# A two-batch attention and expert layer on one core: the stage ahead of the first pair of heads is reordered

## The reference

```
n  = layernorm(x)
q, k, v = n @ wq, n @ wk, n @ wv              # 16 heads of 64
s  = q k^T + bias[bucket(key - query), head]  # 2048 x 2048 for each batch and head
a  = softmax(s) v @ wo
x  = x + layernorm(a)
f  = layernorm(x);  gates = top-2 softmax of mean(f) @ gate_w^T + gate_b
x  = x + layernorm(sum over 8 experts of gate_e * gelu(f @ expert_w_e^T + expert_b_e))
```

## Time and profile before

| | us |
|---|---|
| median of 3 runs | 3034.44 (3033.16 to 3037.01) |
| profiled execution | 3035.34 |
| its span | 3033.6 |
| PE busy | 2843.5 (94%) |
| POOL busy | 2276.8 (75%) |
| DVE busy | 1852.2 (61%) |
| ACT busy | 1663.9 (55%) |

### The profile page before, as it was taken

How to read it: one execution, slowest core, us unless ns; L and a number is a source line. 1 busy time by engine, 2 the same in 40 slices (tenths; PEclk the granted TensorE clock), 3 DMA queues, 4 the chain that set the end, 5 groups by cost and what they waited for, 6 DMA issues and landing times.

```text
span 3033.6 us, 49858 instructions
## 1 busy us (share of the span) xinstructions
PE 2843.5 (94%) x18785; PEld 1052.1 (35%) x18785; DVE 1852.2 (61%) x4692; ACT 1663.9 (55%) x2174; POOL 2276.8 (75%) x1033
## 2 busy tenths in 40 slices
PE   3499999999999999999999999999999999988887
PEld 2133333333333333333333333333333333322443
DVE  5465656665566656565666556565656666685676
ACT  2255555555655555555555565556555555566576
POOL 0088888888888888888988888888888888987000
PEclk8599999999999999999999999999999999999998
DMA  7000000000000000000000000000000000100001
GB/s 159 23 1 1 1 1 18 1 1 1 19 1 1 1 3 17 2 1 2 19 2 1 1 19 1 2 1 2 19 1 1 1 8 1 57 1 29 1 1 56
DMA packets 45607, 36.53 MB, mean 12 GB/s; under 512 B 21510, under 2 KB 43782, under 8 KB 45366
## 3 DMA queue, kind: packets, MB, share of 16 engines
q1 hardware_dynamic: 45366, 33.34, 4.2%
HBM read 28.39 MB, written 11.34 MB: 13 GB/s over the span
## 4 chain that ended last, share of the span: by engine, by line
PE 48%; DVE 20%; issue 18%; POOL 9%; ACT 4%; DMA 1%; SPq 1%; POOLq 0%; DVEq 0%; ACTq 0%
PE po L617 16%; PE st L587 14%; POOL acc L527 9%; PE pre L599 5%; DVE mpart L1265 4%; PE pm L555 4%; DVE st L1282 3%; PE st L817 3%; DVE pre L1262 3%; PE pm L561 2%; DVE pre L1257 2%; PE pm L647 2%; ACT prob L896 1%; PE pm L626 1%; DMA t_scratch<-w_scratch 1%
## 5 line engine op out<-in xcount | busy, mean ns | idle before, releaser
L527 POOL TENSOR_TENSOR acc<-acc,prob 128x1024 f32<-128x1024 f32 x896 | 2117.3, 2363 | 388.1 <-ACT prob L896 308.2
L896 ACT ACTIVATE prob<-st 128x1024 f32<-128x1024 f32 x1024 | 1016.6, 1022 | 911.7 <-DVE st L1282 813.8
L617 PE MATMUL po<-prob,v 128*64 128x512 f32 x4096 | 994.9, 606 | 0.0
L587 PE MATMUL st<-qk 64*128 64x512 f16 x6144 | 835.4, 378 | 21.3 <-ACT prob L896 16.7
L1257 DVE CUSTOM_DVE_ANT_0 pre<-pre,ew 128x512 f32<-128x512 f32 x448 | 300.8, 713 | 567.0 <-issue 566.9
L1262 DVE CUSTOM_DVE_ANT_0 pre<-pre,tab 128x512 f32<-128x512 f32 x704 | 475.2, 715 | 147.2 <-issue 147.1
L587 PEld LDWEIGHTS st<-qk 64*128 64x128 f16 x6144 | 293.3, 94 | 349.9 <-ACT prob L896 60.2
L617 PEld LDWEIGHTS po<-prob,v 128*64 128x64 f32 x4096 | 249.0, 136 | 442.0 <-issue 367.5
L587 PE MATMUL st<-eq,ek 64*128 64x512 f16 x2048 | 389.8, 377 | 0.0
L599 PE MATMUL pre<-qk 64*128 64x512 f16 x1600 | 311.9, 386 | 52.9 <-ACT ew L926 19.2
L1265 DVE TENSOR_REDUCE mpart<-pre 128x2 f32<-128x1024 f32 x224 | 274.0, 1223 | 98.4 <-PE pre L599 96.8
(11 more groups left out here) (189 smaller groups left out, 2350.6 us busy)
## 6 DMA issues: line engine op xcount, KB each, us to landing
t_scratch<-w_scratch SPq DMA_DIRECT2D x2, 3072.0 KB
inv_r<-inv SPq DMA_DIRECT2D x260, 1.0 KB, 1.7
y<-x SPq DMA_DIRECT2D x2, 2048.0 KB, 11.5
qk<-x SPq DMA_DIRECT2D x8, 512.0 KB, 5.6
out<-qk SPq DMA_DIRECT2D x8, 512.0 KB, 3.5
w<-w_pairs SPq DMA_DIRECT2D x8, 384.0 KB, 3.7
t2f<-t_scratch SPq DMA_DIRECT2D x8, 384.0 KB, 4.8
t<-t_scratch SPq DMA_DIRECT2D x8, 384.0 KB, 3.2
```

The lines of the kernel that those rows point to most:

```text
L527: nc.gpsimd.tensor_tensor(acc[g % 2][:, :, :], a, prob[:, n % RING, :, :], ALU.add).then_inc(sum_p, 1)
L587: last = nc.tensor.matmul(st[:, 2 * (n % 2) + h, :], w[64 * h:64 * h + 64, :], t[64 * h:64 * h + 64, :], start=(r == 0), stop=(r == len(te ...
L617: last = nc.tensor.matmul(po[64 * h:64 * h + 64, :], v[:, g // CHUNKS, j, 64 * h:64 * h + 64], prob[:, n % RING, h, :], start=(s == 0), st ...
L896: nc.scalar.activation(prob[:, n % RING, :, :], st[:, 2 * (n % 2):2 * (n % 2) + 2, :], ACT.Exp).then_inc(exp_done, 1)
```

## The change

- SP issues the small loads first, then batch 0's x in four parts with a semaphore each, weights and identity. Batch 1's x is issued when the bias by distance has been stored. Of the tables the first pair's two heads are made first, each table by a DMA of its own, and `t2f` is loaded as soon as its own is there; the fourteen other heads follow. The repetition of two heads at the end of each table is no longer made. Waits for the rest of the tables are put in `tables_in` for pairs 0 and 1.
- DVE takes the statistics of batch 0 part by part, and normalises two of its four groups; ACT normalises the other two and all of batch 1 (`first_tokens`, with a bias made by one more small operation). Batch 1's statistics are put between the low parts of batch 0.
- The first four projections are the key chunks, each when its 512 tokens are there, in the banks `pre`, `po` and `pm`, then query chunk 0 in `st`. The other seven (three query, four value chunks) stand behind pieces 1, 3, 5, 7, 8, 9 and 10 (`FILL_ORDER`, `FILL_AT`). Batch 1's transposes, high and low tokens are put between pieces 11 to 15.
- The far rows and the pair table are made ahead of piece 6.
- y is not cleared: group 0's addition is left out, and the first eight groups write y instead of adding to it.
- The columns' sums on ACT and the memsets at the end of each normalisation go.

```diff
+FILL_ORDER = [4, 5, 6, 7, 0, 1, 2, 3, 8, 9, 10, 11]
+FILL_AT = {1: 5, 3: 6, 5: 7, 7: 8, 8: 9, 9: 10, 10: 11}
...
@@ block.sync
-            for b in range(B):
-                sp.dma_start(y[:, TT * b:TT * b + TT, :], x[b, :, :].rearrange("(t p) d -> p t d", p=128)).then_inc(x_in[b], 16)
...
+            sp.dma_start(hot, onehot).then_inc(rel_in, 16)
+            sp.dma_start(rowc[:, :], rows).then_inc(rel_in, 16)
+            for g in range(GROUPS):
+                sp.dma_start(y[:, 4 * g:4 * g + 4, :], x[0, QC * g:QC * g + QC, :].rearrange("(t p) d -> p t d", p=128)).then_inc(x_part[g], 16)
             sp.dma_start(w3[:, :, :, :].rearrange("p n k c -> p (n k c)"), w_pairs[0, :, :]).then_inc(w_in, 16)
+            sp.dma_start(ident[:, :], eye).then_inc(ident_in, 16)
+
+            def table_out(n, first, heads, done):
+                src = w_scratch[:, n, 127:127 + BAND]
+                src = bass.AP(src.tensor, src.offset + 1024 * first, [[1024, heads], [-1, 128], [1, BAND]])
+                sp.dma_start(t_scratch[n, first:first + heads, :, :], src).then_inc(done, 16)
+
+            sp.wait_ge(dist_out, 2)
+            sp.dma_start(w_scratch, by_dist).then_inc(scratch_out, 16)
+            sp.dma_start(y[:, TT:2 * TT, :], x[1, :, :].rearrange("(t p) d -> p t d", p=128)).then_inc(x_in, 16)
+            sp.wait_ge(scratch_out, 16)
+            table_out(1, 0, 2, first_out)
+            sp.wait_ge(first_out, 16)
+            sp.dma_start(t2f[:, :, :], t_scratch[1, 0:2, :, :].rearrange("h p u -> p h u")).then_inc(t2_in, 16)
+            table_out(0, 0, 2, first_out)
...
             for n in range(2):
-                for to, heads in ((0, H), (H, 2)):
...
+                table_out(n, 2, H - 2, tables_out)
...
@@ block.tensor
+            pe.wait_ge(ident_in, 16)
+            transposes(0, 0)
+            transposes(0, 1)
...
+            for n in range(4):
+                pe.wait_ge(xh_a, KT * (n + 1))
+                pe.wait_ge(xl_v, KT * (n + 1))
+                first_fill(n)
+                if n < 2:
+                    transposes(0, n + 2)
+            first_fill(4)
...
             for u in range(PIECES):
                 piece(0, 0, u)
+                if u in FILL_AT:
+                    first_fill(FILL_AT[u])
+                if 11 <= u < 15:
+                    if u == 11:
+                        pe.wait_ge(v_a, 4)
+                    transposes(1, u - 11)
...
@@ block.scalar
+            ln_sqrt(0)
             split_weights(0)
-            for b in range(B):
-                ln_sqrt(b)
-                high_tokens(b)
-            for f in range(FILLS):
-                high(0, f, st[:, f % 4, :], 0)
+            high_tokens(0, 0)
+            first_tokens(0, 2)
+            high_tokens(0, 1)
+            first_tokens(0, 3)
+            first_high(0)
+            high_tokens(0, 2)
+            first_high(1)
+            high_tokens(0, 3)
+            for n in (2, 3, 4):
+                first_high(n)
+            ln_sqrt(1)
             for u in range(PIECES):
                 rise_of_piece(0, 0, u)
+                if u in FILL_AT:
+                    first_high(FILL_AT[u])
+                if u in (5, 8):
+                    first_tokens(1, u // 8)
+                if 11 <= u < 15:
+                    high_tokens(1, u - 11)
+                if u in (11, 12):
+                    first_tokens(1, u - 9)
...
@@ block.vector, add_output
-                nc.vector.scalar_tensor_tensor(to, bank[:, :], 1.0 / W_UNIT, to, ALU.mult, ALU.add).then_inc(y_add, 1)
+                if G == 0:
+                    dve.nop().then_inc(y_add, 1)
+                elif G <= SLOTS:
+                    nc.vector.tensor_scalar(to, bank[:, :], 1.0 / W_UNIT, None, ALU.mult).then_inc(y_add, 1)
+                else:
+                    nc.vector.scalar_tensor_tensor(to, bank[:, :], 1.0 / W_UNIT, to, ALU.mult, ALU.add).then_inc(y_add, 1)
...
-            nc.vector.memset(y[:, :, :], 0.0).then_inc(y_zero, 1)
...
+            for g in range(GROUPS):
+                dve.wait_ge(x_part[g], 16)
+                for t in range(4):
+                    first_sums(0, 4 * g + t)
+            first_rows(0)
+            for g in range(2):
+                first_tokens(g)
+            low_weights(0)
+            dve.wait_ge(x_in, 16)
+            for g in range(GROUPS):
+                if g == 2:
+                    first_low(0)
+                low_tokens(0, g)
+                if g == 2:
+                    first_low(1)
+                for t in range(4):
+                    first_sums(1, 4 * g + t)
+            for n in (2, 3, 4):
+                first_low(n)
+            first_rows(1)
...
             for u in range(PIECES):
+                if u == 6:
+                    far_rows(0, 0)
+                    pair_table(0, 0)
...
                 piece_max(0, 0, u, first=True)
+                if FILL_AT.get(u, 8) < 8:
+                    first_low(FILL_AT[u])
+                if u >= 12:
+                    low_tokens(1, u - 12)
```

More of the change, by code:

```diff
@@ L286, in layer @@
         consts_in = sem("consts_in")
+        ident_in = sem("ident_in")
+        x_part = [sem(f"x_part{g}") for g in range(TT // 4)]
+        first_out = sem("first_out")
         rel_in = sem("rel_in")
@@ L293, in layer @@
         tables_out = sem("tables_out")
-        x_in = [sem(f"x_in{b}") for b in range(B)]
+        x_in = sem("x_in")
         xr_in = [sem(f"xr_in{b}") for b in range(B)]
@@ L534, in _, with transposes @@
         def _(pe):
[L535 to L547, removed]
+            def transposes(k, g):
+                n = k * GROUPS + g
+                pe.wait_ge(xn_ready, n + 1)
+                if n >= 2:
+                    pe.wait_ge(xh_a, KT * (n - 1))
+                    pe.wait_ge(xl_v, KT * (n - 1))
+                for a in range(KT):
+                    for t in range(4):
+                        last = nc.tensor.transpose(st[:, 2 * (g % 2) + a, 128 * t:128 * t + 128],
+                                                   xn[k % B][:, g % 2, D * t + 128 * a:D * t + 128 * a + 128], ident[:, :])
+                last.then_inc(tr_ready, 1)
             def project(b, f, bank):
@@ L856, in ln_sqrt, with high_tokens, first_tokens @@
                 nc.scalar.activation(std[:, :], var[:, :], ACT.Sqrt).then_inc(ln_sq, 1)
[L858 to L865, removed]
+            def high_tokens(k, g):
+                act.wait_ge(tr_ready, k * GROUPS + g + 1)
+                for a in range(KT):
+                    at = S * (k % B) + 512 * g
+                    act.activation(xh[:, a, at:at + 512], st[:, 2 * (g % 2) + a, :], ACT.Copy).then_inc(xh_a, 1)
+            def first_tokens(b, g):
+                act.wait_ge(lnv, (b + 1) * LN_STEPS)
+                if b == 0:
+                    act.wait_ge(xn_ready, 2)
+                act.wait_ge(tr_ready, b * GROUPS + max(g - 1, 0))
+                for t in range(4):
+                    n = 4 * g + t
+                    last = nc.scalar.activation(xn[b][:, g % 2, D * t:D * t + D], y[:, TT * b + n, :], ACT.Identity,
+                                                bias=newton[:, n:n + 1], scale=rstd[:, n:n + 1])
+                last.then_inc(xn_ready, 1)
             def split_weights(k):
@@ L869, in split_weights, with high @@
                 nc.scalar.activation(wh[:, :, :, :], w3[:, :, :, :], ACT.Copy, scale=W_UNIT).then_inc(w_hi, 1)
-            def high(b, f, bank, P):
-                act.wait_ge(fill, P * FILLS + f + 1)
+            def high(b, f, bank, P, done=None):
+                act.wait_ge(fill, P * FILLS + (f + 1 if done is None else done))
                 if f < 8:
@@ L1145, in _, with first_sums, first_rows @@
         def _(dve):
[L1146 to L1150, removed]
+            def first_sums(b, n):
+                nc.vector.bn_stats(stats[:, n, :], y[:, TT * b + n, :]).then_inc(lnv, 1)
+            def first_rows(b):
+                base = b * LN_STEPS
                 dve.wait_ge(lnv, base + TT)
@@ L1167, in statistics, with first_tokens @@
                 dve.wait_ge(lnv, base + 2 * TT + 5)
+                nc.vector.scalar_tensor_tensor(newton[:, :], mv[:, :, 0], -1.0, rstd[:, :], ALU.mult, ALU.mult).then_inc(lnv, 1)
+                dve.wait_ge(lnv, base + 2 * TT + 6)
+            def first_tokens(g):
+                for t in range(4):
+                    n = 4 * g + t
+                    last = nc.vector.tensor_scalar(xn[0][:, g % 2, D * t:D * t + D], y[:, n, :], mv[:, n, 0:1], rstd[:, n:n + 1],
+                                                   ALU.subtract, ALU.mult)
+                last.then_inc(xn_ready, 1)
             def low_tokens(k, g):
@@ L1232, in pair_table, with low @@
                                             rowc[:, 11:SEL].rearrange("p (c n) -> p c n", c=CHUNKS), one, None, ALU.mult).then_inc(far_add, 1)
[L1234 removed]
+            def low(b, f, bank, P, done=None):
                 t = f % 4
[L1237 removed]
```

(1 more changed line is left out.)

121 lines of the change are left out of this document (44 added, 77 removed).

## The result

The changed kernel takes 2988.51 us (median of 4 runs, 2987.84 to 2989.44) against 3034.23 for the kernel before on the same chip: ratio 0.9848, 95% interval 0.9831 to 0.9865, 45.7 us less. The forecast was 2993, 41.4 less. So the gain is all in the start-up, and the loop behind it gives back 0.6.

The account below looks back on a forecast made before the run. The loop was taken as matmul-bound, so a start-up gain passes whole: 44.0 + 46 + 3.7 and half a microsecond for fetches put the first score at 94 us, 41.4 less, 2993 us; 8 in 10 from 2981 to 3007.

Parts of the forecast that it names:

- first maximum: Start-up, first maximum piece after DVE's mixed stretch: at 44.0 us, 43.1 at full clock, 47.7 at half.
- pieces: The sixteen maximum pieces with work put between them: 46 us, 50 at half clock, 38 at full, 32.2 before.
- row maximum to first score: End of the start-up, row maximum and its DMA up to the first score matmul: 3.7 us.
- first score: First score matmul, end of the start-up: at 94 us against 135.4, a gain of 41.
- first fetches: Start-up: half a microsecond added to the walk for the first fetches.
- Query projections: Three among the maximum pieces, lengthening their cycles: +2.4 us each at half clock, 7.1 in all; 3.6 at full.
- Table: Two far rows and the pair table on DVE ahead of piece 6, nothing over them: +2.5 us.
- Value projections: Four behind pieces 7 to 10: +2.7, +1.3, +1.3 us at half clock; at full hidden but for 0.3.
- Transposes between near pieces: Batch 1's transposes, high and low tokens between the near pieces: +2.9 us, or +2.7 at full clock.
- rival 1: Start-up: work between pieces all hidden, PE at full clock throughout; gain 50.5 us, 2984 us; chance 15%.
- rival 2: Start-up: half clock and late steps; first score at 101 to 107 us, gain 28 to 34, 3000 to 3006; 25%.
- Rival 3: SP's queue: row maximum's DMA waits for the fourteen-head tables; first score 12 us later than before, 3046 us; 3%.

Follow-up runs that it names:

- The parts run alone: Kernel before with only small loads and weights ahead of x: 3027.85 us; only the first pair's table written and loaded first: 3025.16 us; both: 3015.41 us.
- The kept-busy run: Changed kernel with 18 matmuls of 512 columns, whose result nobody reads, put behind piece 0: median 2987.4 us.
- its second trace: Changed kernel run once more with the same instructions, on the chip of three other runs: 2987.72 us, ratio 0.9847 to the kernel before.

## Why the prediction was right

| step | predicted | measured |
|---|---|---|
| DVE starts | 6.0 | 5.80 |
| rows of batch 0 done | 19.2 | 18.6 |
| low weights done | 22.9 | 22.2 |
| first maximum | 44.0 (43.1 to 47.7) | 43.05 |
| pieces | 46 (38 to 50) | 42.2 |
| row maximum to first score | 3.7 | 3.6 |
| first score | 94 | 88.87 |

The mechanism held. DVE sets the pace up to the first reduction; the pieces are a serial chain, longer by what is put between them; and the gain passed through the loop whole (46.0 of 46.6 us). No term was taken from the length of a wait in the profile of before; each was worked out from what would be late next. The parts run alone show why that matters (5 and 8 us alone, 19 together, and 0 for the table in the new order).

Two of the agreements are in part luck. The first maximum was forecast at 43.1 at the full clock and comes at 41.3 to 41.6 in the traces that have it; it is at 43.05 here because the clock was half from 35.5 to 38 us. And the 46 of the pieces is a choice between two prices by feel, not a sum.

The term that was mis-sized is the pieces, by 4 of the 5 us; the rest is the first maximum (0.9) and half a microsecond for first fetches, which no run shows. The base of the pieces was 0.7 too high as well: 32.2 counts from the first piece's matmul at 99.52, but the first maximum is the reduction at 100.27, from which it is 31.5. With that base the measured parts give the 42.2. Query projections: +2.4 each forecast, +2.1 measured at the half clock. Table: +2.5, measured 2.3. Value projections: +5.3 forecast at half clock, measured +1.3, since the clock was full from about 69 us (5.66, 1.8 and 1.8 us for pieces 7 and 8 together, 9 and 10, against 3.91, 2.0 and 2.0). Transposes between near pieces: +2.9 forecast, 11.3 us measured for five against 10.6, so +0.7. In my sum the half clock held for all of it, with 4 us taken off by feel; from the value projections on it was full, as rival 1 had it. That these bring it to full is borne out by the runs: with them between pieces 7 and 11 the matmuls of piece 9 are at the full clock in all six traces (0.39 us), with all projections ahead they are at the half in both (0.61). Rival 1's price (38) was too low, because the first three cycles ran at half, and rival 2's (50) too high, because the last pieces did not. The kept-busy run shows a cycle at the full clock (4.53), the changed kernel one at the half (6.02), and its second trace that the share of each differs from run to run.

Rival 3, the row maximum behind the tables, was off by a lot: the 5.5 MB of the fourteen-head tables were over by 65 us where I had 77, and the DMA engines stood at 0.89 busy with fourteen heads, as fourteen of sixteen would be.

What the forecast did not say, and the runs do: the projections between the pieces are no part of the gain. My own sum priced them at 12.4 us at the half clock (7.1, 2.7 and twice 1.3), and seven projections ahead of the pieces at 1.3 us each would have been 9, but I did not draw the comparison. That the 21 us which are left over come from batch 1's work beside batch 0's and from keys projected as tokens come is a subtraction; neither was undone by itself, and how the 21 us divide between them stays open.

## What to carry to other kernels

Price a part of a start-up by what is late next, and expect two waits that cover each other to give little alone and much together. When work is put between the steps of a serial chain, cut it to the size of the gap, and keep what waits for it behind the chain's own instruction on each engine; whole projections cost what they saved while DVE's low part stood ahead of the reductions, halves of them paid (5.2 us), and moving the low part behind the reductions was worth 5.6 us. Look for an engine's gaps by the brackets of its rows that name another engine, and put there the work that the chain waits for elsewhere.

## What the runs showed of the hardware

- The stop of PE cost twice: its own length of 5.74 us, and the half clock behind it (2.56 instead of 1.29 us from copy to copy), 8.0 us in all.
- In the kernel before the granted clock was 1.00 through the first 18.9 us, in which PE did nothing. In the changed kernel's first trace it fell near 35.3 us, amid back-to-back matmuls that had begun at 34.4; with the same instructions it was still full at 40 us in the second trace. The two traces differ by 2.6 us at the first score.
- Transfers from DRAM to DRAM, split by heads: two heads moved at 51 GB/s with 0.14 of the DMA engines busy, fourteen at 0.89 busy. So the two-head transfer took more time than its bytes alone would.
- A less-to-less cycle with half a projection behind each piece took 3.47 us and one with nothing between the pieces 3.48, both at the full clock.
